# Two attention stages of a decoder kernel: batches in lanes shifted by 6.5 steps, two score banks for each attention

## The chip, the cores and the metric

The kernel runs on one core of a Trainium2 chip. Its engines are TensorE (PE, with its weight loads PEld), VectorE (DVE), ScalarE (ACT), GpSimd (POOL) and SyncE (SP), which here issues the transfers. Each has its own queue of instructions that it works off in order; they wait for each other by semaphores. The metric is the time of one execution in microseconds (us).

## The reference

Two decoder layers on x of shape (8, 128, 256), eight batches of 128 tokens. What the change touches is the first part of layer 0 and the last of layer 1:

```python
# layer 0, self attention: 16 heads of 16, 4 key/value heads, rotary, causal
q, k, v = x @ Wq, x @ Wk, x @ Wv;  q, k = rope(q, k)
x1 = layernorm(x + softmax(causal(q @ k.T) / 4) @ v @ Wo + bo)
# layer 0, cross attention over ctx with compressed keys (64) and queries (96), window by itok
x2 = layernorm(x1 + softmax(window((q_nope @ k_nope.T + q_rope @ k_rope.T) * scale)) @ v @ W_o)
...   # experts of layer 0 and the delta rule of layer 1: not touched
# layer 1, cross attention with int8-valued projections, then a self attention whose
# key and value come from the head that a gate picks
x5 = layernorm(x + w8a8(softmax(w8a8(x) @ k.T / 4 + mask) @ v))
out = layernorm(x5 + softmax(causal(q @ k_best.T) / 4) @ v_best)
```

## The kernel before

Four stages follow each other with barriers between: `layer0_attention` (names with a_), `layer0_experts` (b_), `layer1_delta_rule` (c_) and `layer1_attention` (d_). The change is in the first and the last.

Both work on one batch at a time in each of two lanes, so that two batches are under way: lane 0 has the even ones, lane 1 the odd ones, four for each. A lane has its own buffers and four of the eight PSUM banks, M, S, T and O. A batch of `layer0_attention` goes through: transposes of x and ctx into M (L405, L407) and their copy xcT (L529); the projections into O, M and S (L413 to L424); the rotation of q and k on DVE (`rotate`, L591 to L594) and the spreading of k into kexp on POOL (L382); the key of the cross attention into O (L430) and its rotation; the self attention in four quads of four heads; oT and the output projection y1 (L449, L455); ln1; x1T (L461) and the compressed query (L466); Q in two halves, each of three banks (L477), copied by ACT (L558) and rotated by DVE; the cross attention (L488, L490); latT (L499) and y2 (L506); ln2 and the store.

`Attention` holds the loop over quads, for all attentions: PE writes a mask and the scores of four heads into S, DVE takes the maximum (L179) and writes the difference to pbuf (L184), ACT takes the exponential (L171), PE transposes it into T (L148), ACT copies it to ptbuf (L168), PE multiplies it by the values into O (L156), DVE takes the reciprocal (L190) and scales (L192). There is one bank S, so the scores of a quad are issued only when DVE has read those of the quad before:

```python
                if s >= 1:
                    pe.wait_ge(self.shifted, at(i, QUADS, s))
                scores(s, self.S).then_inc(self.scores_ready, 1)
```

`LayerNorm.on_vector` has two parts, L215 to L224 up to the variance, then, after ACT's square root (L234), L228 and L230. The exponential and the root need different tables of ACT, and a change between them puts an ACT_TABLE_LOAD into its queue.

The order in a queue is that in which the generators are run. `in_turns` runs the programs of both lanes in turns, one piece (up to a `yield`) of lane 0, one of lane 1: the lanes are always at the same step, half a step apart. At its end a lane's program runs `start_batch` of the next batch; on ACT, its first piece comes before the root of ln2.

`layer1_attention` is built alike: ctx transposed (L1874), keys and values (L1880, L1882), `project8` and `scale8` for the quantized projections (L1862, L1867; L2026 to L2031), a cross attention whose mask is added by a float32 product (L1903, L1904), quantizing of its output (L1676 to L1681), a second projection, ln1, x5T (L1913), the gate (L1918) and its choice of a head (L2061 to L2072), q, k and v of all heads (L1922, L1925), the chosen key (krep, L1930, and kexp on POOL, L1835), the self attention (L1938, L1939) and ln2.

Of the kernel before, what the change touches and what calls it, by code (L numbers as in the profile page):

```python
# [13 lines left out]
ALU = mybir.AluOpType  # L14
# [100 lines left out]
class Attention:  # L115
# [17 lines left out]
    def on_tensor(self, pe, i, scores, values):  # L133
# [3 lines left out]
        for s in range(QUADS + 2):  # L137
            if s < QUADS:
                if s >= 1:
                    pe.wait_ge(self.shifted, at(i, QUADS, s))  # L140
                scores(s, self.S).then_inc(self.scores_ready, 1)
# [17 lines left out]
            yield  # L159

    def on_scalar(self, act, i):
        for s in range(QUADS + 1):
            if s >= 1:
# [8 lines left out]
            yield  # L172

    def on_vector(self, dve, i):
        w = self.width + 1
        for s in range(QUADS + 2):
            if s < QUADS:
                dve.wait_ge(self.scores_ready, at(i, QUADS, s + 1))
                dve.tensor_reduce(self.stats[:, 4 * s:4 * s + 4], four(self.S[:, :]), AX.X, ALU.max)\  # L179
# [4 lines left out]
                dve.tensor_tensor(self.p[:, s % 2], four(self.S[:, :]), along(self.stats[:, 4 * s:4 * s + 4], P),  # L184
# [9 lines left out]
            yield  # L194


class LayerNorm:
# [14 lines left out]
    def on_vector(self, dve, i, out, x, y):  # L212
# [13 lines left out]
        yield  # L226
# [16 lines left out]
class Layer0Lane:  # L243


    def __init__(self, nc, ctx, sems, n, ident):
# [31 lines left out]
        banks = (self.S, self.T, self.O)  # L278
# [19 lines left out]
def layer0_attention(nc, sems, d, x_src, x_dst):  # L298

    ctx = ExitStack()  # L300
    with ctx:
# [21 lines left out]
        lanes = [Layer0Lane(nc, ctx, sems, n, ident[:, :]) for n in range(LANES)]  # L323
        xscale = float(np.float32(1.0) / np.sqrt(np.float32(XHD + ROPE)))
# [3 lines left out]
        def _(sp):  # L328
# [9 lines left out]
            for i in range(0, B // LANES - 1):  # L338
                for L in lanes:
                    sp.wait_ge(L.xcT_ps, i + 1)  # L340
                    sp.dma_start(L.ct[:, :], batch(d["ctx"], (i + 1) * LANES + L.n)).then_inc(L.ctx_loaded, 16)
                for L in lanes:
                    sp.wait_ge(L.ln1.step, at(i, L.ln1.DVE_STEPS, 1))
                    sp.dma_start(L.xt[:, :], batch(x_src, (i + 1) * LANES + L.n)).then_inc(L.x_loaded, 16)
                for L in lanes:
                    store_batch(sp, i, i * LANES + L.n, L.ln2.done, L.x2[:, :], x_dst, L.x2_stored, L.x2_free)
            for L in lanes:
                store_batch(sp, B // LANES - 1, B - LANES + L.n, L.ln2.done, L.x2[:, :], x_dst, L.x2_stored, L.x2_free)

        @block.gpsimd  # L350
        def _(pool):
# [22 lines left out]
            for i in range(0, B // LANES):  # L374
                for L in lanes:
# [1776 lines left out]
```

## Time and profile before

| | us |
|---|---|
| median of 3 runs | 2367.83 (2364.08 to 2368.61) |
| profiled execution | 2367.39 |
| its span | 2365.6 |
| first PE work of the batches in `layer0_attention` | 25.6 |
| first instructions of `layer0_experts` | 406.8 |
| first batch in `layer1_attention` | 1989.5 |

Over the whole span PE is busy for 2013.7 us (85%), DVE for 1455.8 (62%), ACT for 879.5 (37%) and POOL for 154.4 (7%). These are averages over four stages that differ; the stretches of the two stages are in the rows further down. A round there is the work on two batches, one in each lane; each stage has four. The times in the timeline are the start and the length of an instruction or of several of one group, and the bracket says how long the engine had been idle and who released it. PE's matmuls are pipelined, so their lengths overlap; the distance between two starts tells what one costs.

### The profile page before, as it was taken

The numbers are of one execution on the slowest core, as the hardware profiler recorded it, in microseconds if no ns is written. First come the engines' busy times: TensorE is split into PE (matmuls) and PEld (weight loads), VectorE is DVE, ScalarE is ACT, GpSimd is POOL, SyncE is SP. The second block draws the span as 40 slices with busy tenths as digits, with TensorE's granted clock in tenths as the row PEclk, the third lists the DMA queues.
The fourth block names the chain that finished last, engine by engine and source line by source line (L and its number), as shares of the span: only waits on it lengthen the run. The fifth ranks groups of instructions, "written<-read, shape, count | busy, mean of one in ns | idle before, by whom it ended". The sixth has DMA issues, their size and how long they took to land. (4 is left out here: it accounts for less than half of the span.)

```text
span 2365.6 us, 27433 instructions
## 1 busy us (share of the span) xinstructions
PE 2013.7 (85%) x10306; PEld 1495.7 (63%) x10306; DVE 1455.8 (62%) x3243; ACT 879.5 (37%) x1540; POOL 154.4 (7%) x143
## 2 busy tenths in 40 slices
PE   6988987998994978899988999889998893787786
PEld 5867866554553667576675766757667582465464
DVE  3667665323222566867668666786666854767666
ACT  2433433111113444353544535535354431333242
POOL 2011011000001000000000000000000002011110
PEclk8989898999996889999999999999999996787787
DMA  3000000400001110201102011020110202000000
GB/s 131 6 14 10 6 5 30 163 1 9 0 1 67 36 36 14 61 16 36 37 14 57 20 37 36 15 60 17 36 36 14 49 1 72 7 12 15 7 5 5
DMA packets 129108, 70.62 MB, mean 30 GB/s; under 512 B 107152, under 2 KB 119504, under 8 KB 127984
## 3 DMA queue, kind: packets, MB, share of 16 engines
q1 hardware_dynamic: 128976, 68.86, 10.2%
q8 instruction: 83, 1.36, 0.2%
q14 instruction: 49, 0.40, 0.1%
HBM read 55.95 MB, written 12.71 MB: 29 GB/s over the span
## 5 line engine op out<-in xcount | busy, mean ns | idle before, releaser
L1249 PE MATMUL c_bank<-c_Y,c_NP 128*128 128x128 f32 x1536 | 179.5, 276 | 20.9 <-ACT c_Y L1404 20.9
L1249 PEld LDWEIGHTS c_bank<-c_Y,c_NP 128*128 128x128 f32 x1536 | 174.9, 192 | 26.5 <-issue 26.5
L1566 DVE TENSOR_TENSOR c_Y<-c_V,c_bank 128x512 f32<-128x512 f32 x192 | 131.7, 686 | 86.0 <-PE c_bank L1249 86.0
L1541 DVE SCALAR_TENSOR_TENSOR c_NP<-c_NP,c_cj,c_bank 128x256 f32<-128x256 f32 x256 | 104.8, 474 | 69.9 <-ACT c_NP L1411 69.9
L1172 PE MATMUL c_bank<-c_xT,c_wqk 128*128 128x512 f32 x256 | 127.3, 644 | 4.1 <-ACT c_pad L1367 3.1
L1502 DVE SCALAR_TENSOR_TENSOR c_cv<-c_pad,c_wcqk,c_cv 128x1024 f32<-128x1024 f32 x96 | 122.2, 1279 | 11.7 <-ACT c_cv L1381 10.9
L1502 DVE SCALAR_TENSOR_TENSOR c_cv<-c_pad,c_wcv,c_cv 128x1024 f32<-128x1024 f32 x96 | 122.5, 1283 | 2.6
L1327 PE MATMUL c_bank<-c_wout,c_yT 128*128 128x256 f32 x512 | 120.6, 381 | 0.0
L1241 PE MATMUL c_bank<-c_NP,c_Tb 128*128 128x256 f32 x512 | 116.3, 383 | 0.0
L1131 POOL TENSOR_TENSOR c_V<-c_Y 128x512 f32<-128x512 f32 x32 | 40.0, 1249 | 1162.4 <-ACT c_Y L1404 1162.4
L1172 PE MATMUL c_bank<-c_xT,c_wv 128*128 128x512 f32 x256 | 112.0, 595 | 4.1 <-DVE c_acc L1594 3.6
L858 ACT ACTIVATE b_sg<-b_G 128x512 f32<-128x512 f32 x50 | 29.8, 597 | 221.6 <-PE b_G L811 221.6
L1232 PE MATMUL c_bank<-c_wz,c_xT 128*128 128x512 f32 x256 | 111.2, 592 | 0.0
L904 DVE TENSOR_TENSOR b_inner<-b_prod,b_R 128x512 f32<-128x512 f32 x44 | 30.3, 688 | 127.0 <-PE b_R L825 127.0
L1241 PEld LDWEIGHTS c_bank<-c_NP,c_Tb 128*128 128x128 f32 x512 | 97.4, 193 | 15.9 <-issue 3.4
L1411 ACT ACTIVATE c_NP<-c_bank,c_gcnR 128x128 f32<-128x128 f32 x256 | 73.2, 368 | 87.1 <-PE c_bank L1195 87.1
L1367 ACT ACTIVATE c_pad<-c_bank 128x512 f32<-128x512 f32 x128 | 69.1, 594 | 93.5 <-PE c_bank L1172 93.5
L1327 PEld LDWEIGHTS c_bank<-c_wout,c_yT 128*128 128x128 f32 x512 | 93.5, 191 | 10.7 <-ACT c_yT L1455 0.2
L811 PE MATMUL b_G<-b_xT,b_wup 128*128 128x512 f32 x200 | 97.6, 612 | 0.0
L811 PE MATMUL b_U<-b_xT,b_wup 128*128 128x512 f32 x200 | 95.4, 600 | 0.0
L1386 ACT ACTIVATE c_qkT<-c_cv 128x1024 f32<-128x1024 f32 x32 | 33.8, 1056 | 162.8 <-DVE c_cv L1502 162.4
L1553 DVE TENSOR_TENSOR c_tmp<-c_A,c_T 128x31 f32<-128x31 f32 (+15 forms) x248 | 84.8, 342 | 15.1 <-DMA c_A<-diagonal_blocks 6.7
(401 smaller groups left out, 4147.3 us busy)
## 6 DMA issues: line engine op xcount, KB each, us to landing
b_wup<-b_in_wup SPq DMA_DIRECT2D x4, 1280.0 KB, 14.3
c_wqk<-c_in_wqk SPq DMA_DIRECT2D x9, 512.0 KB, 3.3
c_wv<-c_in_wv SPq DMA_DIRECT2D x8, 512.0 KB, 3.3
c_wz<-c_in_wz SPq DMA_DIRECT2D x8, 512.0 KB, 4.6
c_wout<-c_in_wout SPq DMA_DIRECT2D x8, 512.0 KB, 3.5
diagonal_blocks<-c_NP SPq DMA_DIRECT2D x64, 64.0 KB, 1.9
c_A<-diagonal_blocks SPq DMA_DIRECT2D x8, 512.0 KB, 3.4
c_NP<-no_blocks SPq DMA_DIRECT2D x32, 128.0 KB, 3.8
```

Of the source, the lines that this page charges most:

```text
L811: last = pe.matmul(bank[:, :], wup[:, t, k, m, :], xT[:, bass.ds(i, 1), m, :].rearrange("p a n -> p (a n)"), start=m == 0, stop=m == DC - 1)
L1172: last = pe.matmul(four(pair[q][:, :]), w[:, c * P:(c + 1) * P], xT[:, c, 4 * q:4 * q + 4, :], start=c == 0, stop=c == DC - 1)
L1232: last = pe.matmul(banks[6 + b % 2][:, :], xT[:, c, b, :], wz[:, c, :], start=c == 0, stop=c == DC - 1)
L1241: last = pe.matmul(banks[u % 4][:, b * 2 * P:(b + 1) * 2 * P], Tb[:, h * B + b0 + b, :], NP[:, h, b0 + b, :, :].rearrange("p a n -> p (a n ...
L1249: last = pe.matmul(banks[n % 4][:, b * P:(b + 1) * P], lhsT(h, 4 * q + b), rhs(h, 4 * q + b), start=True, stop=True)
L1327: last = pe.matmul(banks[2 + m % 2][:, 0:D], yT[:, m % 2, h, :], wout[:, h, :], start=h == 0, stop=h == HB - 1)
L1367: act.activation(pad[:, m % 2, 4 * q:4 * q + 4, TAPS - 1:], four(pair[q][:, :]), ACT.Copy)\
L1411: act.activation(NP[:, h, 4 * q + b, 1, :], banks[4 + n % 2][:, b * P:(b + 1) * P], ACT.Exp, bias=gcnR[:, h, 4 * q + b:4 * q + b + 1]).the ...
L1502: dve.scalar_tensor_tensor(cv[:, m % 2], pad[:, m % 2, :, t:t + S], w, cv[:, m % 2], ALU.mult, ALU.add)\
L1541: dve.scalar_tensor_tensor(NP[:, h, bb, :, :], spread(NP[:, h, bb, 1, :], 2), cj[:, h, bb:bb + 1], gp, ALU.mult, ALU.mult).then_inc(s["NP_ ...
L1553: elim(dve.tensor_tensor(part, along(A[:, j, j + 1:BL], w), spread(T[:, j, 0:w], n), ALU.mult))
L1566: dve.tensor_tensor(rr(Y, h, q), rr(V, h, q), four(banks[n % 4][:, :]), ALU.subtract).then_inc(s["y_ready"], 1)
```

## The change

Each `yield` now gives the number of a step, and `in_step_order` merges the lanes by i * PERIOD + lane * LAG + step, with a period of 24 steps in `layer0_attention` and 28 in `layer1_attention` and a lag of 6.5 steps in both. So the start of a batch follows the end of the one before in the same lane, and the second lane is 6.5 steps behind the first (an attention takes six). All five queues of both stages are ordered so, the transfers on SP (steps .9) and POOL's work among them. An attention has two banks for scores, S and M, and the scores of quad n + 1 are issued before the transposes of quad n - 1; at the first step two quads are issued.

```diff
-def in_turns(programs):
-    done = object()
-    running = list(programs)
-    while running:
-        running = [p for p in running if next(p, done) is not done]
+def in_step_order(lanes, period, lag, program):
+    def steps(n, L):
+        for i in range(B // LANES):
+            for step in program(i, L):
+                yield i * period + n * lag + step
+    running = [[next(p), n, p] for n, p in enumerate(steps(n, L) for n, L in enumerate(lanes))]
+    while running:
+        first = min(running)
+        first[0] = next(first[2], None)
+        if first[0] is None:
+            running.remove(first)
...
-        self.S, self.PT, self.O = banks
+        self.S, self.PT, self.O = banks[0:2], banks[2], banks[3]
...
-    def on_tensor(self, pe, i, scores, values):
+    def on_tensor(self, pe, i, scores, values, step):
         for s in range(QUADS + 2):
-            if s < QUADS:
-                if s >= 1:
-                    pe.wait_ge(self.shifted, at(i, QUADS, s))
-                scores(s, self.S).then_inc(self.scores_ready, 1)
+            if s:
+                yield step + s
+            for n in ((0, 1) if s == 0 else (s + 1,)):
+                if n < QUADS:
+                    if n >= 2:
+                        pe.wait_ge(self.shifted, at(i, QUADS, n - 1))
+                    scores(n, self.S[n % 2]).then_inc(self.scores_ready, 1)
...
-        banks = (self.S, self.T, self.O)
+        banks = (self.S, self.M, self.T, self.O)
...
+        PERIOD, LAG = 24, 6.5
...
+            def batch_program(i, L):
+                yield from start_batch(i, L)
+                yield 3
...
                 for half in range(2):
-                    if half:
+                    yield 14 + half
+                    if half == 0:
+                        pe.wait_ge(L.qc_ready, i + 1)
+                    else:
                         pe.wait_ge(L.Qa_ready, at(i, 4, 2))
                         pe.wait_ge(L.Qr_ready, at(i, 4, 2))
...
-            in_turns([start_batch(0, L) for L in lanes])
-            for i in range(0, B // LANES - 1):
-                in_turns([lane_program(i, L, True) for L in lanes])
-            in_turns([lane_program(B // LANES - 1, L, False) for L in lanes])
+            in_step_order(lanes, PERIOD, LAG, batch_program)
...
-                next_start = start_batch(i + 1, L)
-                next(next_start)
-                yield
+                yield 24
                 L.ln2.on_scalar(act, i)
-                yield from next_start
...
+        PERIOD, LAG = 28, 6.5
```

Three places show what this does to the queues. In the rows a0 is lane 0 and a1 lane 1 of `layer0_attention`; the numbers of lines in the kernel after are some 5 to 20 higher.

PE, where Q is projected, before:

```order
L466 MATMUL a1_M<-a1_x1T,a_wdq 96x128 x2
L477 MATMUL a0_M<-a0_qcT,a_wabs 128x128 x4
L477 MATMUL a0_S<-a0_qcT,a_wqr 128x128 x4
L477 MATMUL a0_T<-a0_qcT,a_wqr 128x128 x4
L477 MATMUL a1_M<-a1_qcT,a_wabs 128x128 x4
L477 MATMUL a1_S<-a1_qcT,a_wqr 128x128 x4
```

PE at the same place after:

```order
L495 MATMUL a0_T<-a0_qcT,a_wqr 128x128 x4
L165 MATMUL a1_O<-a1_vaug,a1_ptbuf 128x17 x4
L495 MATMUL a0_M<-a0_qcT,a_wabs 128x128 x4
L495 MATMUL a0_S<-a0_qcT,a_wqr 128x128 x4
L495 MATMUL a0_T<-a0_qcT,a_wqr 128x128 x4
L468 MATMUL a1_M<-a_ident,a1_osb 128x128 x2
L506 MATMUL a0_S<-a0_segb,a_identb 128x512
L508 MATMUL a0_S<-a0_key,a0_Q 128x128 x4
```

Before, lane 1's half of Q stood between the two halves of lane 0; now one O product of lane 1 stands there, and two transposes between the second half and lane 0's cross scores.

DVE, at the end of the cross attention of lane 0, before:

```order
L192 TENSOR_TENSOR a0_lat<-a0_O,a0_stats 128x256
L190 RECIPROCAL a1_stats<-a1_O 128x4
L192 TENSOR_TENSOR a1_lat<-a1_O,a1_stats 128x256
L215 TENSOR_TENSOR a0_ln2_sum<-a0_x1,a0_T 128x256
L216 BN_STATS a0_ln2_stats<-a0_ln2_sum 128x6
```

DVE after, at the sum of the same ln2:

```order
L190 TENSOR_REDUCE a1_stats<-a1_S 128x4
L195 TENSOR_TENSOR a1_pbuf<-a1_S,a1_stats 128x512
L225 TENSOR_TENSOR a0_ln2_sum<-a0_x1,a0_T 128x256
L226 BN_STATS a0_ln2_stats<-a0_ln2_sum 128x6
...
L190 TENSOR_REDUCE a1_stats<-a1_M 128x4
L195 TENSOR_TENSOR a1_pbuf<-a1_M,a1_stats 128x512
L238 RECIPROCAL a0_ln2_rstd<-a0_ln2_rstd 128x1
```

The ln2 of lane 0, which waits for y2, now stands between quads 0 and 1 of lane 1's cross attention.

ACT, around ln1 in `layer0_attention`, before:

```order
L234 ACTIVATE a_ln_rstd<-a_ln_rstd 128x1 x2
L549 ACTIVATE a_x1T<-a_M 128x256 x2
L552 ACTIVATE a_qcT<-a_M 96x128 x2
L558 ACTIVATE a_Q<-a_M 64x4x128 x8
L171 ACT_TABLE_LOAD
```

ACT after:

```order
L178 ACTIVATE a_ptbuf<-a_T 128x512
L181 ACTIVATE a_pbuf<-a_pbuf 128x512
L244 ACT_TABLE_LOAD
L244 ACTIVATE a_ln_rstd<-a_ln_rstd 128x1
L178 ACTIVATE a_ptbuf<-a_T 128x512
L181 ACT_TABLE_LOAD
L181 ACTIVATE a_pbuf<-a_pbuf 128x512
```

Before, both lanes' roots stood together, between two attentions; now each stands alone between two exponentials of the other lane. In the whole queue the loads for exponentials and roots of these two stages go from 30 to 62.

## Rows read from the trace of the kernel before

**Rows 1.** Round: length, busy of PE, PEld, DVE, ACT, POOL; then granted clock, DMA.
```profile
119.60:213.80 94.20, 83.47 (x571) 72.30 (x570) 62.92 (x147) 36.64 (x70) 9.01 (x6) 0.89 0.03 9
2082.00:2175.00 93.00, 72.14 (x337) 49.41 (x337) 63.15 (x180) 31.17 (x58) 13.04 (x8) 0.78 0.03 11
```

**Rows 2.** Waits of PE: us in total, times, longest; the first, then the last stage.
```profile
PE a_S L442 <- DVE a_key L594: 22.2, 4, 5.7
PE a_M L461 <- DVE a_x L230: 11.4, 4, 3.3
PE a_S L488 <- DVE a_Q L594: 7.1, 8, 1.5
...
PE d_M L1913 <- DVE d_x L230: 22.5, 4, 5.6
...
PE d_M L1930 <- DVE d_krep L2084: 10.4, 4, 2.6
```

**Rows 3.** Timeline (start us, us, engine, line): PE in a self attention of layer 0.
```profile
150.67 0.38 PE L442 MATMUL a_S<-a_causalb,a_identb 128*128 128x512 bf16 x1
...
151.74 0.60 PE L148 MATMUL a_T<-a_ident,a_pbuf 128*128 128x128 f32 x4
...
152.99 0.38 PE L442 MATMUL a_S<-a_causalb,a_identb 128*128 128x512 bf16 x1
```

**Rows 4.** Groups by line and shape in 119.6 to 213.8: busy us, mean ns.
```profile
L184 DVE TENSOR_TENSOR a_pbuf<-a_S,a_stats 128x512 f32<-128x512 f32 x16 | 11.1, 691 | 0.5
L179 DVE TENSOR_REDUCE a_stats<-a_S 128x4 f32<-128x512 f32 x16 | 11.0, 689 | 3.8 <-PE a_S L443 2.1 <-PE a_S L490 1.3
L171 ACT ACTIVATE a_pbuf<-a_pbuf 128x512 f32<-128x512 f32 x16 | 10.1, 630 | 19.6 <-DVE a_pbuf L184 19.6
```

**Rows 5.** Timeline: the halves of Q on PE and a rotation on DVE.
```profile
174.62 0.69 DVE L591 TENSOR_TENSOR a_t<-a_S,a_xrope 128x512 f32<-128x512 f32 x1 [6.67 <-PE a_T L477]
...
175.24 1.06 PE L477 MATMUL a_S<-a_qcT,a_wqr 96*128 96x128 f32 x8
...
176.07 1.40 DVE L594 TENSOR_TENSOR a_Q<-a_t 64x512 f32<-64x512 f32 x2
176.14 1.06 PE L477 MATMUL a_T<-a_qcT,a_wqr 96*128 96x128 f32 x8
...
177.62 1.13 PE L477 MATMUL a_M<-a_qcT,a_wabs 96*128 96x128 f32 x8 [0.43 <-DVE a_Q L594]
```

**Rows 6.** Timeline: table load and root of a layernorm, and its part on DVE.
```profile
122.66 1.28 ACT L234 ACT_TABLE_LOAD   x1
...
123.95 0.20 ACT L234 ACTIVATE a_ln_rstd<-a_ln_rstd 128x1 f32<-128x1 f32 x1
...
163.29 0.42 DVE L215 TENSOR_TENSOR a_ln_sum<-a_xt,a_M 128x256 f32<-128x256 f32 x1 [2.68 <-PE a_M L455]
...
165.06 0.20 ACT L234 ACTIVATE a_ln_rstd<-a_ln_rstd 128x1 f32<-128x1 f32 x1 [1.98 <-DVE a_ln_rstd L224]
```

**Rows 7.** Timeline: y2 of both lanes on PE, and the ln2 that waits for it.
```profile
206.50 7.07 PE L506 MATMUL a_T<-a_wuvo,a_latT 128*128 128x256 f32 x32
...
210.16 0.42 DVE L215 TENSOR_TENSOR a_ln_sum<-a_x,a_T 128x256 f32<-128x256 f32 x1 [4.64 <-PE a_T L506]
```

**Rows 8.** Timeline: kexp on POOL and the rotation of the key on DVE.
```profile
135.04 5.70 POOL L382 TENSOR_TENSOR a_kexp<-a_qk,a_own_block 128x1024 f32<-128x1024 f32 x3 [3.43 <-DVE a_qk L594]
...
135.52 3.46 DVE L594 TENSOR_TENSOR a_key<-a_t 64x128 f32<-64x128 f32 x2
```

**Rows 9.** Timeline: masks of two quads that follow each other, layer 1's cross attention.
```profile
2110.16 1.10 PE L1903 MATMUL d_S<-d_mask,d_ident 128*128 128x512 f32 x2
...
2113.21 1.10 PE L1903 MATMUL d_S<-d_mask,d_ident 128*128 128x512 f32 x2
```

**Rows 10.** Busy time by stretch, columns as in rows 1: two stretches of 4 us.
```profile
155.60:159.60 4.00, 4.00 (x39) 4.00 (x36) 1.61 (x9) 1.71 (x3) 0.00 (x0) 0.97 0.02 4
159.60:163.60 4.00, 3.97 (x13) 2.97 (x13) 0.71 (x3) 2.05 (x3) 0.00 (x0) 0.50 0.00 0
```

More of the change, by code:

```diff
@@ L158, in on_tensor, with on_scalar @@
                 last.then_inc(self.o_ready, 1)
-            yield
-    def on_scalar(self, act, i):
+    def on_scalar(self, act, i, step):
         for s in range(QUADS + 1):
+            if s:
+                yield step + s
             if s >= 1:
@@ L210, in __init__, with on_vector @@
         self.done = ph.sem(name + "_done")
-    def on_vector(self, dve, i, out, x, y):
+    def on_vector(self, dve, i, out, x, y, then):
         link = Linked(dve, self.step, self.DVE_STEPS, i)
@@ L507, in lane_program @@
                 last.then_inc(L.y2_ps, 1)
-                yield
-                if more:
-                    yield from start_batch(i + 1, L)
-            in_turns([start_batch(0, L) for L in lanes])
-            for i in range(0, B // LANES - 1):
-                in_turns([lane_program(i, L, True) for L in lanes])
-            in_turns([lane_program(B // LANES - 1, L, False) for L in lanes])
+            in_step_order(lanes, PERIOD, LAG, batch_program)
         @block.scalar
@@ L1724, in __init__ @@
         self.xquant = Quantizer(ph, "xquant", 2)
-        banks = (self.S, self.T, self.O)
+        banks = (self.S, self.M, self.T, self.O)
         self.cross_att = Attention(ph, "cross", HD, banks, self.pbuf, self.ptbuf, self.stats, self.osb, ident)
@@ L1855, in _, with project8 @@
             pe.wait_ge(s["wstep_ready"], 1)
-            def project8(i, L, n, out):
-                yield
+            def project8(i, L, n, out, step):
+                yield step
                 pe.wait_ge(L.xquant.done, at(i, 2, n + 1))
@@ L1891, in start_batch, with batch_program @@
                 last.then_inc(L.qT_ps, 1)
-                yield
-            def lane_program(i, L, more):
+            def batch_program(i, L):
+                yield from start_batch(i, L)
+                yield 5
                 pe.wait_ge(L.qT_ready, i + 1)
@@ L1993, in lane_program @@
                 act.wait_ge(L.qkv_ps, i + 1)
                 act.activation(L.qT2[:, :, :], half(L.T[:, 0:D]), ACT.Copy, scale=0.25).then_inc(L.qT2_ready, 1)
[L1995 removed]
+                yield 19
                 act.wait_ge(L.krepT_ps, i + 1)
                 act.activation(L.krepT[:, :], L.M[:, 0:P], ACT.Copy).then_inc(L.krepT_ready, 1)
[L1998 to L2003 removed]
@@ L2004, in lane_program @@
-                next_start = start_batch(i + 1, L)
-                next(next_start)
-                yield
-                L.ln2.on_scalar(act, i)
-                yield from next_start
-            in_turns([start_batch(0, L) for L in lanes])
-            for i in range(0, B // LANES - 1):
-                in_turns([lane_program(i, L, True) for L in lanes])
-            in_turns([lane_program(B // LANES - 1, L, False) for L in lanes])
+                yield 20
+                yield from L.self_att.on_scalar(act, i, 20)
```

293 lines of the change are left out of this document (139 added, 154 removed).

## The prediction

> **What bounds the kernel now.** I read the busy times by stretch first, then PE's waits, then the timeline of one round, row by row. Two of the four stages are touched: the layer 0 attention stage, from 25.6 us to the start of the next at 406.8 (381 us), and the layer 1 attention stage, from 1989.5 us to the end (376 us); the 1583 us between stay as they are. A round of two batches takes 94.2 us in the first stage and 93.0 us in the last [rows 1]. In the first, PE is busy for 83.5 us of a round, DVE for 62.9; in the last 72.1 and 63.2. So in the first stage PE is close to being the bound, in the last none is: there the dependency chain of a batch sets the pace. PE's waits say where: in the four rounds of stage one 22.2 us before the first scores of the self attention, 11.4 before the transposes of x1, 7.1 before the cross scores; in the last stage 22.5 before the transposes of x5 and 10.4 before that of krep [rows 2]. Within an attention there is hardly one: the same four pieces of PE come again every 2.32 us, once for each lane and quad, with no gap between them [rows 3]. The second bank for scores cannot gain there, PE is full already.
>
> **How I cost the new order.** Each engine has one fixed queue, and the change writes all of them anew, so the question is the time of one period: 24 steps in stage one, 28 in the last, each for two batches, as a round was. I walked the new queues of PE, ACT and DVE through one period, each operation at its duration in the trace at full clock, and noted each gap on PE.
>
> What PE has to do in a period of stage one: 16 lane-quads at 2.32 to 2.4 us make 38 us; 12 banks of Q projection at 0.90 us (from 175.24 to 176.14) 10.8 [rows 5]; y2 7.1 [rows 7]; all else about 19. That is 75 us. The shift would give 94 - 75 = 19 us a round if nothing waited. The gaps that I find in its place:
>
> 1. *Q projections.* A half of Q writes M, S and T, and its rotation on DVE takes 2.85 us (174.62 to 177.47) [rows 5]. Before, the other lane's 2.7 us half ran meanwhile, and PE waited 0.4 us there. Now only one lane is at that step, and behind its first half stand the last O product of the other lane (0.8 us), and then the second half, which waits for the rotation: a gap of 2.3 us. Behind the second half stand two transposes, then the cross scores, which wait for the second rotation: 2.8 us. The other lane's pair gives 2.2 and 2.2. Sum 9.5 us, against 0.4 + 1.8 before.
> 2. *First layernorm.* It is 1.77 us on DVE up to the square root (163.29 to 165.06), then a table load of 1.28 and the root of 0.20 on ACT [rows 6], then 0.6 on DVE. On DVE this sits between quads 0 and 1, and between 1 and 2, of the other lane's attention, and its first operation waits for y1, which PE has behind two quads of scores. A lone lane's chain, maximum and subtraction 1.38 and exp 0.63 [rows 4], already fills 2.0 of the 2.32 us, so it cannot absorb 4 us. PE's gaps: 2.1 + 0.6 + 1.9 for one lane, 1.9 + 0.4 + 1.9 + 0.3 for the other, together 9.1, against 11.4 / 4 = 2.9 before.
> 3. *Second layernorm and the next start.* DVE reaches the sum of ln2 before the second quad of the other lane's scores, and y2 needs 3.53 us (half of 7.07) [rows 7], so DVE stands and a queued maximum behind it too. With root, table, the copy of xcT and the rotation of the key, gaps of 1.4 + 0.35 + 2.6 + 0.85 for lane 0 and 2.35 + 0.85 + 3.4 for lane 1: 11.8 us, against 22.2 / 4 = 5.6. The last 3.4 us is an old one: the two operations of the key's rotation took 3.46 us beside the GpSimd's kexp [rows 8], and both the attention behind them on DVE and the lane's scores wait for it.
>
> Sum 30.4 us of gaps on 75: a period of 105 us, against 94.2. Table loads are in it: the queue of ACT has 62 for exp and root now where it had 30, 32 more at 1.28 us, 41 us of ACT, a part of which lies in items 2 and 3. The Trainium skill, ScalarE: Activation LUTs, "What ACT_TABLE_LOAD costs", puts a drain of about 1.38 us behind each load of 1.28. Here the root starts 0.01 us after the load has ended (122.66 + 1.28 to 123.95) [rows 6], so the trace does not agree; with the page's price and half of the 32 extra loads on the path the sum would be 22 us higher.
>
> **The ends of a stage.** Lane 1 starts and ends 6.5 steps behind. For 6.5 steps at each end one lane runs alone: I get 24 us at the start (the projections, the key beside kexp, three quads) and 21 at the end (three cross quads, y2, layernorm, store). The 89.5 steps between are 3.73 periods. Stage one: 24 + 21 + 3.73 x 105 = 437 us, 56 more than 381.
>
> **The last stage**, same walk. The cross quad is 3.05 us of PE (2110.16 to 2113.21) [rows 9]; PE's work is 8 x 3.05 + 8 x 2.32 + 14 = 57 us a period, so there is more room and the shift fits better: the quantizing, the projection and the root of one lane do fall beside the other's quads, and the long waits before x5T (5.6 us a round) and the start go. What stays is the chain from the logits to the self scores, in which DVE has both the end of one lane's attention and the other's choice of a head: gaps of 4.7 and 4.4 us before the self scores, and nine of 1 to 2 us. The period comes out at 89 us. With 13 us at the start, 15 at the end and 105.5 / 28 = 3.77 periods: 28 + 335 = 363, 13 less than 376.
>
> **Clock.** All of this is at 2.4 GHz, as if granted throughout; before, the mean grant is 0.89 and 0.78 [rows 1]. It can fall without an idle PE: in the 4 us up to 159.6 PE is busy for all of them and has 0.97, in the next it has 0.50 though busy for 3.97 [rows 10]. Nothing in the trace shows the new mixture of scores, short O products and gaps of 2 us. Lower bound: no loss, 0 us. Upper bound: the grants of before with nothing of it hidden, 75 x (1/0.89 - 1) = 9 us a period in stage one and 57 x (1/0.78 - 1) = 16 in the last, 34 + 60 = 94 us in all. I take a quarter of it, 2 and 4 us a period, since before most of the stretches at 1.2 GHz lay where PE had little to do: 7.5 + 15 = 22 us.
>
> DMA: the ctx and xt loads are issued over ten steps before they are needed, the store's wait on SP has 3 us of nothing behind it: nothing. GpSimd does the same work; nothing beyond item 3.
>
> Sum against the profiled execution of 2367.4 us (its span 2365.6; the median of the runs is 2367.8, the same): +56 - 13 + 22 = +65, so 2432 us. A measurement of this kernel can tell about 0.2%, 5 us, from no change.
>
> **Rivals.** *PE packs after all* (faster). My gaps are sums of hops in one fixed order; where a queue stands 1 us earlier than I have it, several of them close at once. For it speaks that the work is only 75 and 57 us; against it, that each gap hangs on a written wait and not on a tight race. With periods of 85 and 80 us: 45 + 317 = 362 and 28 + 302 = 330, -19 - 46, so 2302. It turns the sign once stage one's period is below 90 or so.
> *The stages cancel.* Half of the excess gaps in stage one (96) and a last stage at 84: 45 + 358 = 403, 28 + 317 = 345; +22 - 31, so 2358.
> *The clock stays low* in both stages (the upper bound above): 2367 + 43 + 94 = 2504. For it: item 1 to 3 break PE's work every few us. Against: none of the gaps is over 5 us, and before, an attention got its full grant within a few us.
>
> **Chances.** My forecast 0.63 (its own range 2395 to 2475), packs 0.12, cancel 0.12, low clock 0.13. Faster: the 0.12 and 0.07 of the second, 0.19; within 0.2% 0.04; slower 0.77. The range 2350 to 2490 leaves out the first rival and half of the last.
>
> **What would show it.** After: in stage one PE waits for a_Q before the second Q half and before the cross scores, some 2 to 3 us each, sixteen and more times; DVE waits 2 to 3 us for y2 while maxima stand behind it; a period of about 105 us, one of about 90 to 95 in the last stage; 1.28 us table loads between the exps. I am wrong if DVE's and PE's waits in stage one sum to less than before, or if the last stage's PE clock is under 0.7.

## The result and the profile after

The changed kernel takes 2531.28 us, the median of 4 runs (2522.7 to 2537.75), against 2367.94 (2364.08 to 2368.61) before: slower by 7.09%, ratio 1.0709 with an interval of 1.0685 to 1.0732. The forecast was slower, 2432 us, with a range of 2350 to 2490. So the sign was right, and the time lies 41 us above the upper end. Every stage length below is from one profiled execution; that of after is 2537.75 us, its span 2536.0, and so the slowest of the four, 6.5 us over their median.

The page of the kernel after, the first rows; digits are tenths in 40 slices of the span:

```profile
span 2536.0 us, 27478 instructions
...
PE 2104.3 (83%) x10306; PEld 1559.9 (62%) x10306; DVE 1435.3 (57%) x3243; ACT 916.1 (36%) x1572; POOL 152.6 (6%) x143
...
PEclk8787878769999788999999999999999996877777
```

PE runs the same 10306 products, yet is busy for 2104 us instead of 2014. Busy time by stretch of the first and the last stage, each from its first transpose of a batch to its end; columns as in rows 1. Before:

```profile
25.58:406.80 381.22, 329.86 (x2240) 286.31 (x2240) 249.74 (x580) 145.60 (x279) 36.04 (x24) 0.89 0.03 8
1989.54:2365.60 376.06, 285.98 (x1336) 194.65 (x1336) 251.12 (x720) 123.53 (x231) 52.14 (x32) 0.77 0.03 9
```

After:

```profile
26.43:548.91 522.48, 398.13 (x2240) 344.40 (x2240) 242.63 (x580) 164.85 (x295) 36.02 (x24) 0.79 0.02 6
2132.56:2536.00 403.44, 307.85 (x1336) 200.61 (x1336) 237.80 (x720) 140.79 (x247) 50.50 (x32) 0.78 0.03 8
```

The first stage is 141 us longer, the last 27, and all else 2 (1610.1 instead of 1608.3 us). In the first stage PE's idle time is 124 us (522.5 - 398.1) instead of 51, so 73 us of the loss are waits. The other 68 are busy time: the same 2240 products take 398 us instead of 330, while the granted clock falls from 0.89 to 0.79 of 2.4 GHz. Laid over the records of the products, 1.2 GHz covers 63 of the 330 busy us before and 191 of the 398 after. At that level a product takes twice as long (a bank of Q 1.85 us instead of 0.90), so it costs 32 and 95 us: 64 of the 68. In the last stage 22 of the 27 us are busy time; 1.2 GHz covers 115 of 286 us before and 142 of 308 after, which makes 13 of the 22.

One period of each stage, from a store of lane 0 to its next one (147.23 to 273.47 us; 2224.26 to 2323.11):

```profile
147.20:273.50 126.30, 98.35 (x562) 85.50 (x562) 60.37 (x148) 41.48 (x75) 8.99 (x6) 0.80 0.02 7
2224.30:2323.10 98.80, 76.33 (x334) 49.93 (x334) 58.82 (x181) 35.39 (x63) 12.57 (x8) 0.79 0.03 10
```

PE's waits in the first stage after (us in total, times, longest us):

```profile
PE a_T L157 <- ACT a_pbuf L181: 29.1, 18, 2.3
PE a_S L460 <- DVE a_key L600: 20.4, 8, 5.7
PE a_S L506 <- DVE a_Q L600: 19.1, 8, 2.6
PE a_M L495 <- DVE a_Q L600: 18.3, 8, 2.3
PE a_M L506 <- DVE a_pbuf L195: 12.8, 8, 1.8
PE a_M L460 <- DVE a_pbuf L195: 7.3, 4, 1.8
```

In the last stage the long waits before x5T are gone (22.5 us before, 6.9 after), and the longest in sum is for kexp of GpSimd. Before, then after:

```profile
PE d_S L1938 <- POOL d_kexp L1835: 2.1, 4, 0.9
```

```profile
PE d_S L1950 <- POOL d_kexp L1844: 19.4, 8, 2.4
```

And PE's timeline at the Q projections of lane 0:

```profile
209.95 1.73 PE L165 MATMUL a_O<-a_vaug,a_ptbuf 128*128 128x17 f32 x8
211.52 2.05 PE L495 MATMUL a_M<-a_qcT,a_wabs 96*128 96x128 f32 x8
213.37 1.91 PE L495 MATMUL a_S<-a_qcT,a_wqr 96*128 96x128 f32 x8
215.07 1.32 PE L495 MATMUL a_T<-a_qcT,a_wqr 96*128 96x128 f32 x8
...
219.50 2.05 PE L495 MATMUL a_M<-a_qcT,a_wabs 96*128 96x128 f32 x8 [2.31 <-DVE a_Q L600]
221.34 1.91 PE L495 MATMUL a_S<-a_qcT,a_wqr 96*128 96x128 f32 x8
...
228.00 0.59 PE L506 MATMUL a_S<-a_segb,a_identb 128*128 128x512 bf16 x1 [2.61 <-DVE a_Q L600]
```

The gaps of 2.31 and 2.61 us are those of item 1 of the prediction. What it did not have is the pace of the banks: 1.70 to 1.85 us from start to start where it was 0.90 [rows 5]. The granted clock by stretches of 4 us says why:

```profile
203.60:207.60 4.00, 2.12 (x19) 1.78 (x17) 2.95 (x8) 3.54 (x6) 0.00 (x0) 1.00 0.00 0
207.60:211.60 4.00, 4.00 (x27) 3.94 (x25) 0.92 (x3) 1.99 (x4) 0.00 (x0) 0.65 0.02 4
211.60:215.60 4.00, 4.00 (x20) 4.00 (x20) 0.41 (x2) 0.00 (x0) 0.00 (x0) 0.50 0.00 0
215.60:219.60 4.00, 1.69 (x16) 1.62 (x15) 2.97 (x6) 1.18 (x2) 0.00 (x0) 0.93 0.00 0
219.60:223.60 4.00, 4.00 (x19) 4.00 (x20) 0.11 (x1) 0.00 (x0) 0.00 (x0) 0.50 0.00 0
```

PE is busy all through the second and third stretch and gets 0.65 and 0.50, that is 1.2 GHz in the third; in the last stretch it is the same. Ahead of each fall PE had stood still for about half of a stretch (busy for 2.12 and 1.69 of 4 us) at or near the full clock. In rows 10 of before the clock fell after a stretch in which PE was busy throughout. The low clock now lies where PE has the most to do.

### The profile page after: what moved, and what is told of

Read it like the earlier page. It is cut to its first block and busy times, and to the rows that moved or that the text cites. A ratio compares the mean times of both kernels' runs of the same rounds, so it can differ in the third digit from the quotient of the medians.

```text
span 2536.0 us, 27478 instructions
## 1 busy us (share of the span) xinstructions
PE 2104.3 (83%) x10306; PEld 1559.9 (62%) x10306; DVE 1435.3 (57%) x3243; ACT 916.1 (36%) x1572; POOL 152.6 (6%) x143
## 5 line engine op out<-in xcount | busy, mean ns | idle before, releaser
L1254 PE MATMUL c_bank<-c_Y,c_NP 128*128 128x128 f32 x1536 | 179.5, 276 | 20.9 <-ACT c_Y L1409 20.9
L863 ACT ACTIVATE b_sg<-b_G 128x512 f32<-128x512 f32 x50 | 29.8, 597 | 220.5 <-PE b_G L816 220.5
L840 PE MATMUL b_Y<-b_wdown,b_inner 128*128 128x256 f32 x400 | 93.8, 379 | 0.0
```

The lines of the kernel that those rows point to most:

```text
L840: last = pe.matmul(Y[b // 2][:, b % 2 * D:(b % 2 + 1) * D], inner[:, n % 2, b * P:(b + 1) * P], wdown[:, n, :], start=False, stop=n == ECH ...
L1254: last = pe.matmul(banks[n % 4][:, b * P:(b + 1) * P], lhsT(h, 4 * q + b), rhs(h, 4 * q + b), start=True, stop=True)
```

## The experiments

Two theories. *Gaps and clock*: the gaps are as walked, and they make the clock fall, which lengthens PE's own work. *Gaps alone*: a wait somewhere is longer than walked, and the clock has little to do with it. Inside both, the question is which part of the change makes the gaps: the shift, the early scores, the second bank or the table loads. All stage lengths, PE busy times and clocks are from the profiled executions:

| kernel | us, median | first stage | PE busy | clock | last stage | PE busy | clock |
|---|---|---|---|---|---|---|---|
| before | 2368 | 381.2 | 329.9 | 0.89 | 376.1 | 286.0 | 0.77 |
| after | 2531 | 522.5 | 398.1 | 0.79 | 403.4 | 307.9 | 0.78 |
| e1 new first stage alone | 2500 | 521.9 | 397.7 | 0.79 | 374.4 | 284.4 | 0.77 |
| e3 lag 0.5 | 2378 | 380.1 | 333.0 | 0.88 | 391.1 | 296.0 | 0.74 |
| e4 one bank | 2514 | 485.2 | 371.4 | 0.84 | 412.1 | 297.0 | 0.80 |
| e5 busy at two places | 2519 | 500.8 | 407.9 | 0.83 | 402.8 | 306.2 | 0.78 |
| e6 busy at six places | 2497 | 486.2 | 418.3 | 0.92 | 404.0 | 309.8 | 0.77 |
| e7 lag half a period | 2423 | 436.3 | 356.5 | 0.85 | 370.5 | 287.2 | 0.78 |
| e8 scores not early | 2486 | 468.1 | 364.5 | 0.85 | 404.8 | 308.9 | 0.78 |
| e9 no root table | 2473 | 478.0 | 368.3 | 0.85 | 380.0 | 299.9 | 0.79 |
| e10 before, no root table | 2362 | 381.5 | 329.9 | 0.89 | 372.6 | 283.2 | 0.77 |
| e11 lags 0.5 and 14.5 | 2359 | 384.0 | 336.2 | 0.88 | 370.0 | 283.0 | 0.79 |
| e12 the same, busy | 2349 | 375.5 | 349.0 | 0.93 | 363.2 | 317.4 | 0.86 |
| e13 lag 9.5 | 2432 | 433.6 | 353.1 | 0.86 | 391.4 | 306.7 | 0.77 |
| e14 busy at six, not early | 2488 | 466.4 | 404.0 | 0.95 | 402.9 | 308.1 | 0.78 |
| e15 as e12, not early | 2343 | 366.5 | 333.4 | 0.96 | 360.2 | 312.4 | 0.88 |
| e16 no root table, not early | 2423 | 448.9 | 355.0 | 0.87 | 365.2 | 288.0 | 0.82 |

Ratios are given against the runs of before made with each (medians of 2361.6 to 2365.6). A stage length of a single execution is uncertain by some us: the same first stage took 380.1 in e3 and 384.0 in e11, and the profiled executions lie up to 10 us beside the medians of their kernels (after 6.5 over, e5 6.0 and e14 9.7 under). Where that matters the difference of the medians stands beside it.

**e1, the two stages apart.** The last stage and its classes are those of before:

```diff
-        banks = (self.S, self.M, self.T, self.O)
+        banks = (self.S, self.T, self.O)
...
-            in_step_order(lanes, PERIOD, LAG, batch_program)
+            in_turns([start_batch(0, L) for L in lanes])
```

> Layer 0 attention as after (two banks, step order, lag 6.5), layer 1 attention as before. Reading of the two traces: the first stage went from 381 to 523 us, the last from 376 to 405. If the stages do not touch each other: 2368 + 142 = 2510 us, and the last stage back at 376. Rival: part of the loss in the last stage is carried over from the first (a chip that has been throttled earlier); then the last stage stays near 400 here and the time is near 2530.

Measured: 2499.8 us, ratio 1.0583 (1.0549 to 1.0617). The last stage is back at 374.4 us, so nothing is carried over from the first: the two losses are separate.

**e3, no shift.**

```diff
-        PERIOD, LAG = 24, 6.5
+        PERIOD, LAG = 24, 0.5
...
-        PERIOD, LAG = 28, 6.5
+        PERIOD, LAG = 28, 0.5
```

> As after, but the second lane only half a step behind in both stages: two score banks, scores a step ahead and the step order stay, the shift goes. Theory A, the shift is the whole cause (it puts a lone lane's waits and the table loads between the quads of the other, and these let PE's clock fall): about the time of before, 2350 to 2390, with a granted clock of 0.88 or more in the first stage and 16 us or less of its idle time in front of the Q rotations. Theory B, the early scores or the next start behind the last root cost by themselves: 2430 or more.

Measured: 2377.8, ratio 1.0066 (1.0049 to 1.0083). The first stage is as before (380.1 us); its waits for the Q rotations shrink from 37.4 to 4.4 us. So in the first stage the whole loss needs the shift. The last stage stays 15 us above before even without it: the next start no longer lies ahead of the last root, or the early scores cost there. Which of the two wasn't separated.

**e4 and e8, the banks and the early issue.** One bank, scores as before:

```diff
-            for n in ((0, 1) if s == 0 else (s + 1,)):
+            for n in (s,):
                 if n < QUADS:
-                    if n >= 2:
-                        pe.wait_ge(self.shifted, at(i, QUADS, n - 1))
-                    scores(n, self.S[n % 2]).then_inc(self.scores_ready, 1)
+                    if n >= 1:
+                        pe.wait_ge(self.shifted, at(i, QUADS, n))
+                    scores(n, self.S[0]).then_inc(self.scores_ready, 1)
```

> As after with its shift of 6.5 steps, but with one score bank and each quad's scores behind the subtraction of the quad before, as before the change. A lone lane's chain through PE is then scores, maximum and subtraction 1.38, next scores. Theory A, the second bank gains little: 2531 to 2560. Theory B, the second bank is what keeps the shifted lanes from waiting for each other (some 0.6 us for each of 128 lane-quads): 2600 or more. Below 2520 would say that the second bank itself does harm.

Measured: 2514.5, ratio 1.0646 (1.0618 to 1.0675), faster than the full change, which neither theory had as its case. Below 2520 I had meant to blame the second bank itself; e8 shows that it isn't to blame. In the first stage two banks with early scores cost 37 us against one bank; in the last they gain 9. For both stages together that is 29 us, by the medians of the whole kernel 17. e8 takes the early issue alone away:

```diff
-            for n in ((0, 1) if s == 0 else (s + 1,)):
+            for n in (s,):
```

> As after (shift 6.5, two score banks), but quad n's scores are issued at step n as before the change, not a step early. With one bank and no early scores the first stage took 485 us, with both 522. Theory A, the early issue is what costs (the scores stand before the transposes in PE's queue and wait there for the subtraction, with everything of the other lane behind): 475 to 490 us. Theory B, the second bank itself (M has other uses, so its readers hold up the scores): 515 to 525. For the last stage, where one bank took 412 and two early 403: A says it goes with the early issue, 410; B 403.

Measured: 2486.0, ratio 1.0509 (1.0485 to 1.0533); the first stage takes 468.1 us, lower than theory A's 475. So the second bank gains 17 us there and the early issue loses 54 (by the medians of the whole kernel 45). Of the 54, 34 are busy time (398.1 to 364.5) and 20 are waits. The waits that go are those of the early scores for the subtraction:

```profile
PE a_T L157 <- ACT a_pbuf L181: 24.8, 26, 1.5
PE a_S L460 <- DVE a_key L600: 21.0, 8, 5.7
PE a_S L506 <- DVE a_Q L600: 18.4, 8, 2.8
PE a_M L495 <- DVE a_Q L600: 17.6, 8, 2.3
PE a_M L479 <- DVE a_x L240: 5.5, 8, 0.7
```

After's `L506` and `L460` on M, 12.8 + 7.3 us, have no row here, and the longest wait for an exp is 1.5 us instead of 2.3. In the last stage the early issue gains 1 us only, and the second bank 7 (412.1 to 404.8), where theory A had given the early issue the whole gain.

**e5 and e6, the clock.** PE gets more to do. e5 adds the products at the two waits for the Q rotations, e6 also at four more places of a batch; the products write the lane's idle bank O:

```diff
+            def keep_busy(L, count):
+                for _ in range(count):
+                    pe.matmul(four(L.O[:, :]), identb[:, :], spread(causalb[:, :], 4), start=True, stop=True)
...
                     else:
+                        keep_busy(L, 8)
                         pe.wait_ge(L.Qa_ready, at(i, 4, 2))
...
                 yield 16
+                keep_busy(L, 8)
                 pe.wait_ge(L.seg_step, at(i, 4, 4))
```

> As after, with extra matmuls that nobody reads in the first stage: before each half-Q's wait for the rotation and before the cross scores, eight bf16 products of 128x512 into the lane's idle O bank (128 in all, 0.21 us each at 2.4 GHz, 27 us of added PE work). Theory A, the clock: PE's instructions of the first stage take 398 us instead of 330 since the gaps before the Q rotations and around them pull the granted clock from 0.89 to 0.79; filled gaps bring the clock back, 0.82 or more, and the stage is no longer than after's 522 us though PE has more to do, 500 to 522. Theory B, the gaps alone: what the filling adds beyond the gaps (2.3 and 2.8 us for the first lane, 2.2 for the second, so 0 to 1.9 each at the low clock) comes on top, 525 to 545 us, at the same clock of 0.79.

> As the run before, with eight such products also at four more places of each batch in the first stage: twice between y1 and the transposes of x1, before the first projections, and before y2 (384 products of 0.21 us in all, 81 us of PE work). Theory A (clock): a granted clock of 0.9 or more, and a stage of 522 us or less, since the low clock costs 85 us there. Theory B (the gaps alone): most of the 81 us shows, 560 us or more.

Measured: e5 2519.2, ratio 1.0664 (1.0631 to 1.0698), e6 2496.5, ratio 1.0557 (1.0535 to 1.0578). The first stage takes 500.8 and 486.2 us instead of 522.5, though PE has 128 and 384 products more. e5's clock of 0.83 and e6's 0.92 and both lengths are theory A's. By the medians e6 is 35 us under after, clear of the noise; e5 is 12 under, and its interval touches that of after. PE in e5 at a Q projection of which the first half has no extra products ahead of it:

```profile
231.15 2.02 PE L500 MATMUL a_M<-a_qcT,a_wabs 96*128 96x128 f32 x8
232.96 1.91 PE L500 MATMUL a_S<-a_qcT,a_wqr 96*128 96x128 f32 x8
234.66 1.31 PE L500 MATMUL a_T<-a_qcT,a_wqr 96*128 96x128 f32 x8
235.81 1.00 PE L165 MATMUL a_O<-a_kvaug,a_ptbuf 128*128 128x65 f32 x8
236.65 1.89 PE L418 MATMUL a_O<-a_causalb,a_identb 128*128 128x512 bf16 x8
239.08 1.13 PE L500 MATMUL a_M<-a_qcT,a_wabs 96*128 96x128 f32 x8 [0.54 <-DVE a_Q L606]
```

The first half's banks are 1.81 us apart, as in after; behind the extra products one takes 1.13 us instead of 2.02. The cross scores, which follow such products in every batch, go from 347 ns a product to 275 in the stage's groups. In e6 extra products stand ahead of the first half too. The groups of the Q projection over the first stage (busy us, mean ns), before, after and e6:

```profile
L477 PE MATMUL a_S<-a_qcT,a_wqr 96*128 96x128 f32 x128 | 18.2, 289 | 0.0
```

```profile
L495 PE MATMUL a_S<-a_qcT,a_wqr 96*128 96x128 f32 x128 | 27.2, 385 | 0.0
```

```profile
L418 PE MATMUL a_O<-a_causalb,a_identb 128*128 128x512 bf16 x384 | 97.3, 399 | 0.0
...
L504 PE MATMUL a_S<-a_qcT,a_wqr 96*128 96x128 f32 x128 | 16.9, 275 | 0.0
```

That is the low clock as a cause, not a companion: nothing was taken away, the same products are shorter, and the stage is 36 us shorter.

An estimate of the first stage at full clock follows from e6. The added products at its clock take 81 / 0.92 = 88 us; with the 68 us still idle (486.2 - 418.3) that makes 156, against 124 idle in after, so 32 us of them overrun their gaps. Without these 454; PE's own 330 us at 0.92 would be 304 at 1.0, so 428 us. The walk said 437.

**e14, the early issue with the clock held up.** The edit is that of e6 and that of e8 together.

> The run with extra matmuls at six places of a batch in the first stage (486 us there, clock 0.92), but with quad n's scores at step n, as in the run without early scores (468 us, clock 0.85, against 522 and 0.79). Theory A, the early issue costs mostly through the clock, as its waits break PE's work into pieces: with the clock held up it makes a small difference, 475 to 486 us. Theory B, its waits are gaps of their own on the path: 486 - 40 or more, 446 us or less.

Measured: 2488.2, ratio 1.0513 (1.0488 to 1.0538), the first stage 466.4 us in an execution that is 9.7 us faster than the median. Where the clock is held up the early issue costs 20 us by the stages (486.2 to 466.4) and 8 by the medians, with intervals that touch; where it isn't, 54 and 45. By the stage it falls between the two theories, by the medians it is theory A's; either way more than half of the loss came through the clock. Even here the clock differs (0.92 and 0.95), so what is left isn't all waits.

**e9, e10 and e16, the table loads.** The layernorms take the exponential for the root, so no other table is needed between the exps; the output isn't that of the reference.

```diff
-        act.activation(self.rstd[:, 1:2], self.rstd[:, 0:1], ACT.Sqrt).then_inc(self.root_ready, 1)
+        act.activation(self.rstd[:, 1:2], self.rstd[:, 0:1], ACT.Exp).then_inc(self.root_ready, 1)
```

> As after, but the layernorms of the two attention stages take ACT's exponential where they took its square root (the output is then not that of the reference), so that no table is loaded between the exps: 32 loads of 1.28 us go that the change had added, and the 30 of before. Theory A, the loads lie in the gaps of the first layernorm and the next start (my items 2 and 3): 25 to 60 us less than after, 2470 to 2505, with part of it from a better clock. Theory B, the loads are beside other work: 2520 or more.

> The kernel before, with the exponential in place of the square root in the layernorms of the two attention stages (output not that of the reference), so without their table loads. In the kernel after this took 44.5 us off the first stage (522.5 to 478.0) and 23 off the last (403.4 to 380.0). Theory A, the loads that the shift adds are most of that: here 10 to 25 us in both stages together, since one load for exp and one for root serve both lanes; so 45 to 60 us of the 170 lost by the change are the table's. Theory B, the loads weigh the same in both kernels: 50 us or more here.

> After with exponential for root in both attention stages (output not that of the reference) and with quad n's scores at step n. Alone, the first took the first stage from 522 to 478 us, the second to 468. Theory A, they are the same gaps (the exp of a lone lane comes late because of the table, and the early scores' wait stands before the transposes that wait for it): 455 to 468. Theory B, they are separate: 522 - 44 - 54 = 424.

Busy time by stretch, both stages, e9 and then e10:

```profile
26.38:504.42 478.04, 368.31 (x2240) 317.16 (x2240) 242.90 (x580) 125.20 (x264) 36.05 (x24) 0.85 0.02 6
2088.89:2468.90 380.01, 299.93 (x1336) 197.18 (x1336) 238.50 (x720) 99.92 (x216) 50.56 (x32) 0.79 0.03 9
```

```profile
26.04:407.52 381.48, 329.93 (x2240) 286.49 (x2240) 249.96 (x580) 126.13 (x264) 36.01 (x24) 0.89 0.03 8
1988.35:2360.90 372.55, 283.23 (x1336) 192.73 (x1336) 251.24 (x720) 103.98 (x216) 52.10 (x32) 0.77 0.03 9
```

ACT has 31 instructions fewer in each stage of the changed kernel and 15 fewer in each of before: these are the loads. e9: 2472.9, ratio 1.0465 (1.0444 to 1.0487); without its loads the changed kernel is 68 us shorter by its stages, 44.5 in the first and 23 in the last (58 by the medians). e10: 2361.8, ratio 0.9986 (0.9977 to 0.9995), only 3 or 4 us, below even theory A's 10. There one pair of loads serves both lanes, at a step where neither has an exp to do. In the first stage the 44.5 us are 30 of busy time and 15 of waits; here too most goes through the clock.

e16, with the early issue gone too: 2423.2, ratio 1.0245 (1.0224 to 1.0265), the first stage 448.9. Apart the two give 54 and 44.5, together 74, between the 54 to 67 and the 98 expected. So a quarter of their sum is the same microseconds. In the last stage it is the other way: apart the loads take 23 us and the early issue gains 1, but once the loads are gone the early issue costs 15 (380.0 to 365.2). Its 365.2 us are 7 less than e10's 372.6: there the shift with a second bank gains, were it not for the loads and the early scores.

**e7 and e13, other lags.**

```diff
-        PERIOD, LAG = 24, 6.5
+        PERIOD, LAG = 24, 12.5
...
-        PERIOD, LAG = 28, 6.5
+        PERIOD, LAG = 28, 14.5
```

> As after, but shifted by half a period: 12.5 steps in the layer 0 attention, 14.5 in the last stage. In the first stage one lane's self attention then stands beside the other's cross attention for all of its six steps, and the projections and layernorms beside each other. Theory A (gaps arise where one lane's attention meets the other's projections and layernorms): the period returns towards 94 to 105 us in the first stage, its clock to 0.85 or more; with 12.5 steps of one lane alone at each end, about 430 us for the stage and 2430 to 2480 in all. Theory B (any shift is bad, whatever stands beside what): 2530 or more.

e13 has 9.5 in both places.

> As after with a lag of 9.5 steps in both stages. Lane 0's three Q steps then stand between quads 2 to 4 of lane 1's self attention, where with 6.5 only an O product stood. Theory A (what a gap meets decides): the waits before the Q rotations, 30 to 37 us in the stage with 6.5, fall to half; the stage lands between the 522 us of lag 6.5 and the 436 of 12.5, at 450 to 490. Theory B (the length of the lag decides through the ends): 522 + 3/24 of a period of 126, 538 us.

Measured: e7 2423.4, ratio 1.0253 (1.0233 to 1.0273), below the 2430 to 2480 expected; e13 2432.2, ratio 1.0282 (1.0258 to 1.0307). With half a period the first stage takes 436.3 us at a clock of 0.85, and the last 370.5, less than before. With 9.5 steps the first takes 433.6, less than I expected. PE's waits there:

```profile
PE a_M L479 <- DVE a_x L240: 15.2, 4, 3.8
PE a_S L460 <- DVE a_key L600: 14.9, 8, 5.7
PE a_M L495 <- DVE a_Q L600: 14.4, 8, 3.1
PE a_S L506 <- DVE a_Q L600: 9.1, 5, 3.0
...
PE a_T L157 <- ACT a_pbuf L181: 3.9, 7, 0.8
```

The Q waits fall from 37.4 to 23.5 us, and those for an exp from 29.1 to 3.9. So what counts is what a lane's steps meet in the other lane, not how long the lag is: 9.5 and 12.5 steps have longer ends than 6.5 and lose less.

**e11, e12 and e15, a version that beats both.** e11 takes for each stage the lag that did best (0.5 and 14.5). e12 adds products that nobody reads, e15 takes the early issue away again:

```diff
                 yield 3
+                if L.n == 0:
+                    pe.wait_ge(L.qk_ready, i + 1)
+                    keep_busy(pe, L.S, identb, causalb, 14)
                 pe.wait_ge(L.kr_ready, at(i, 2, 2))
...
                 yield 12
+                if L.n == 0:
+                    keep_busy(pe, L.O, identb, causalb, 10)
                 pe.wait_ge(L.ln1.done, i + 1)
...
                 yield 4
+                pe.wait_ge(L.kT_ready, at(i, DC, DC))
+                keep_busy(pe, L.S, identb, causalb, 8)
                 pe.wait_ge(L.yb_ready, at(i, 2, 1))
...
                 yield 15
+                keep_busy(pe, L.O, identb, causalb, 12)
                 pe.wait_ge(L.ln1.done, i + 1)
...
                 yield 19
+                keep_busy(pe, L.S, identb, causalb, 6)
                 pe.wait_ge(L.krep_ready, i + 1)
```

> As after, with the lag chosen for each stage: half a step in the first (380 us there with this lag), 14.5 steps in the last (370.5 us). If the stages are independent: 2362 - 1 - 6 = 2355 us, faster than before by some 0.2 to 0.3%. If the run with both at 14.5 and 12.5 steps owed its last stage to the first: 2362 or more.

> As the run before, with products of 128x512 in bf16 that nobody reads, put where PE waits long: in the first stage 10 before the transposes of x1 and 14 before the self scores, for lane 0 alone; in the last stage 12 before the transposes of x5, 8 before those of q and 6 before that of krep, for every batch. Granted clock there without them 0.88 and 0.78. Theory A (the clock follows what PE does in the gaps): above 0.92 and 0.85; PE's own work then shrinks by some 10 and 20 us, while the products overrun some gaps; 2325 to 2350 us. Theory B: in this order the low clock lies where PE has little to do, so nothing is won and the overrun shows: 2355 to 2380.

> The version with a lag for each stage and extra matmuls (375.5 and 363.2 us for the stages, 2349 in all), with quad n's scores at step n. Theory A, where both lanes' attentions meet each quad's scores have a whole step of the other lane behind them, so issuing early gains nothing: within 5 us, 2344 to 2354. Theory B, the early issue pays in the lanes that fit: 2358 or more. If it harms there as it does at 6.5 steps: under 2342.

Measured: e11 2359.4, ratio 0.9973 (0.9961 to 0.9985); e12 2348.8, 0.9924 (0.9910 to 0.9939); e15 2342.7, 0.9900 (0.9883 to 0.9916), 1.0% faster than before. e15 by stretch:

```profile
26.88:393.37 366.49, 333.42 (x2336) 283.12 (x2336) 241.84 (x576) 145.78 (x279) 36.02 (x24) 0.96 0.03 8
1980.18:2340.40 360.22, 312.36 (x1544) 201.99 (x1544) 239.33 (x720) 125.59 (x233) 50.75 (x32) 0.88 0.03 9
```

With 96 and 208 products more than before, the stages are 15 and 16 us shorter, at clocks of 0.96 and 0.88 instead of 0.89 and 0.77. The clean test of the products is e12 against e11: 384.0 to 375.5 and 370.0 to 363.2 us, 11 us in all by the medians, with intervals that are apart. Taking the early issue away (e15 against e12) gives 6 us more by the medians, just below the 2344 to 2354 of theory A, but the intervals touch; the 9 and 3 us of the stages are too many, as the untouched middle was 6 us longer in that execution. So that the early issue is a loss here too is likely and not shown. Why PE's clock is lower with it where the lanes stand in step (0.93 against 0.96) stays open.

## Why the prediction was right in its sign and wrong in its size

**What bounds the kernel.** Right: the kernel is slower, since PE had no room in the first stage. With their shares of the clock I had the first stage 63.5 us longer and the last 2; they are 141 and 27 longer. That the second bank "cannot gain there, PE is full already" held only for lanes in step. In shifted lanes the bank gains 17 us (e4 to e8) and the early issue loses 54 (45 by the medians). I never priced the early issue by itself; its waits were in my gaps, its effect on the clock wasn't.

**The gaps.** Right in the first stage, too many in the last. In a period of the first stage PE is idle for 126.30 - 98.35 = 28.0 us; walked were 30.4. Item 1 gave 9.5 us a period; the two waits for a_Q are 19.1 + 18.3 = 37.4 us in four periods, 9.35 each, sixteen times in all. Items 2 and 3 gave 20.9; what is left of the 28.0 is 18.6. DVE's waits for y2 came, 8 times, with 31.0 us in all rather more than the 2 to 3 us each; but the trace of before has them too, 8 times and 25.7 us, so they tell little. In the last stage the gaps are 98.80 - 76.33 = 22.5 us, fewer than the 32 that I walked (89 - 57). That GpSimd adds "nothing beyond item 3" was wrong there: PE waits 19.4 us for kexp, before 2.1.

**PE's own work at full clock.** Right. Laid over PE's records in the two periods, 1.2 GHz covers 45.7 of 98.35 busy us and 34.5 of 76.33. With half of that taken off, 75.5 and 59.1 us are left, for the 75 and 57 walked.

**The clock. This is the step that failed.** I took 2 and 4 us a period. Measured are the halves of 45.7 and 34.5: 22.8 and 17.3. (Busy time times the mean clock would give 19.7 and 16.0; that is too low, since the waits got a higher clock than the work.) So the first stage's period of 126.3 us, 21.3 over the 105 walked at full clock, is 22.8 of clock, 0.5 of PE's sum and 2.4 less of gaps, to within 0.4; the last one's 98.8, 9.8 over its 89, is 17.3 + 2.1 - 9.5, to within 0.1. Over 3.73 and 3.77 periods the clock took 85 + 65 = 150 us instead of the 22 in the sum. That is 128 too little. The profiled execution missed the forecast by 106 us only, since the gaps were 45 too many, while PE's sum (10) and the ends (9) were too low.

Two things in the trace of before spoke against a quarter. A round there already lost 7.1 and 14.9 us to the clock (1.2 GHz over 14.3 and 29.8 of its busy us), so 2 and 4 meant that the change would raise the clock, and the 105 at full clock was set against 94.2 with that loss in it. And the reason given, that the stretches at 1.2 GHz lay where PE had little to do, is not so: PE was busy for 63 of the 87 us at 1.2 GHz in the first stage and for 115 of the 171 in the last.

**The rival "clock stays low"** (2504, chance 0.13) was nearest to what came true, and even its bound was too low: it took the grants of before, 9 us a period in the first stage, where the change itself pushed them down. My argument against it, that none of the gaps is over 5 us, looked at the wrong thing: from 203.6 to 223.6 us PE waited for 2.31 us at most at a time, and the clock was granted at 1.00, 0.65, 0.50, 0.93 and 0.50. The Trainium skill, TensorE: Matmul & The Clock Gate, "A second HAM failure mode: psum-queue depth-cycling", tells of such a case in another kernel: PE pausing for very short times between groups of products, often enough that the clock swings between its two levels. I had not weighed it as a rival. The clocks just named agree with it.

**The ends.** 522.5 - 3.73 x 126.3 = 51 us and 403.4 - 3.77 x 98.8 = 31, for 45 and 28.

**The table loads.** Inside the walk at full clock, but they cost more than their own time on the path: 68 us by the stages with them against without (e9), against 3 or 4 in before (e10), and 38 of the 68 are PE's busy time (30 in the first stage, 8 in the last). The further drain behind each load, which the Trainium skill, ScalarE: Activation LUTs, "What ACT_TABLE_LOAD costs", puts at 1.38 us, was rightly left out of the sum: the trace of after has the load at 202.98 for 1.28 us and the root at 204.27. That doesn't make the loads cheap.

**What would show it.** The signs that I named came: the waits for a_Q, for y2, the loads between the exps. The period in the last stage was 98.8, above "90 to 95", and the one in the first 126 instead of 105. The condition on the clock stood on the wrong stage: I asked that the last one stay over 0.7, which it did (0.78), and said nothing of the first, where it fell.

## What to carry to other kernels

Where PE is near its limit, price a new order by what it does to PE's granted clock, and not only by the gaps (here no wait ahead of the falls shown was over 2.31 us); start from what the clock costs in the kernel as it is, and as an upper bound take the low clock over all work that lies next to a gap, a bound that no run here tests. A wait written ahead of ready work in an in-order queue (scores issued early, ahead of transposes) can cost more than it hides once the lanes are out of step. And a clock that is low for want of steady work can be bought back by products that nobody reads, put where the engine waits anyway.

## What the runs showed of the hardware

- More products can make a stage shorter: 384 of 128x512 in bf16, 81 us at full rate, took it from 522.5 to 486.2 us and the clock from 0.79 to 0.92. In e12 they are 96 and 208, and the kernel is 0.4% faster than e11 without them (2348.8 against 2359.4).
- The low clock does not lie only where PE idles: 211.60 to 215.60 is recorded as fully busy and got 0.50. Waits bring the clock down: e9 has the same products in the same order on PE, and only its waits are shorter (110 us idle instead of 124); its clock is 0.85 instead of 0.79. They are not ahead of every fall: in rows 10 PE was busy for all of the 4 us ahead of it, with transposes and O products of 17 columns. Whether such narrow products bring the clock down by themselves no run told apart.
- Table loads between the exps of the other lane cost 44.5 and 23 us in a stage with 31 of them, 40 us of ACT's time at 1.28 each. Where both lanes reach the root together, 15 loads cost 0 and 3.5 us.
